# The second layer of a four-block transformer stack run in halves of two blocks, with layer norm and expert routing placed between expert tiles

## What is computed

```
x = x + 0.5 * ffn0(norm(x));  x = x + mamba(norm(x));  x = x + 0.5 * ffn0(norm(x))
x = x + 0.5 * moe(norm(x));   x = x + attention(norm(x));  x = x + 0.5 * moe(norm(x))

def moe(x):                       # 64 experts of width 88, top 8 of 64
    scores = sigmoid(x @ gate_w.T)            # [T, 64]
    # 8 groups of 8 experts; a group's value is the sum of its two best
    # keep the 4 best groups, then the 8 best experts, weights normalised * 2.5
    rw = route(scores, gate_bias)             # [T, 64], zero but for 8
    out = sum_e rw[:, e] * (silu(x @ Wg[e].T) * (x @ Wu[e].T)) @ Wd[e].T
    return out + shared(x)                    # one always-on expert, width 176
```

## Time and profile before

| | |
|---|---|
| time, three runs | 1789.91, 1790.04, 1793.42 us; median 1790.04 |
| the profiled execution | time 1788.16 us, span 1786.4 us |
| busy over the span | PE 1614.6 us (90%), DVE 1227.8 (69%), ACT 955.5 (53%), POOL 897.1 (50%) |
| mean granted PE clock | 0.947 of 2.4 GHz |
| DMA | 118.72 MB in 30035 packets |
| F1, mixer, F2 | 0 to 631.2 us of the span |
| E1 | 631.2 to 1070.7 |
| attention | 1070.7 to 1334.6 |
| E2 | 1334.6 to 1786.4 |

### The profile page before, as it was taken

How to read it: one execution, slowest core, us unless ns; L and a number is a source line. 1 busy time by engine, 2 the same in 40 slices (tenths; PEclk the granted TensorE clock), 3 DMA queues, 4 the chain that set the end, 5 groups by cost and what they waited for, 6 DMA issues and landing times.

```text
span 1786.4 us, 25495 instructions
## 1 busy us (share of the span) xinstructions
PE 1614.6 (90%) x6840; PEld 1208.8 (68%) x6840; DVE 1227.8 (69%) x2015; ACT 955.5 (53%) x1866; POOL 897.1 (50%) x786
## 2 busy tenths in 40 slices
PE   8997577787899975999999998999998699999998
PEld 6775323333377754888888876898875488888887
DVE  5555699999755564666666666787766466666666
ACT  4344645454334342565656555777763256556565
POOL 1001076666410042777777773434323277777776
PEclk9998789999899987999999998999997699999999
DMA  2000000000000003666667640000000367767765
GB/s 102 10 0 1 0 1 1 0 0 0 7 1 1 0 36 84 147 150 152 146 154 150 144 105 1 1 0 0 0 10 1 91 144 152 152 147 152 148 150 120
DMA packets 30035, 118.72 MB, mean 66 GB/s; under 512 B 5323, under 2 KB 17059, under 8 KB 18211
## 3 DMA queue, kind: packets, MB, share of 16 engines
q1 hardware_dynamic: 29987, 118.15, 29.8%
HBM read 116.03 MB, written 2.10 MB: 66 GB/s over the span
## 4 chain that ended last, share of the span: by engine, by line
PE 66%; DVE 3%; issue 2%; POOL 2%; ACT 2%; DMA 1%; POOLq 0%; DVEq 0%; SPq 0%; ACTq 0%
PE ps L219 19%; PE ps L220 18%; PE ps L221 18%; PE ps L1292 2%; PE ps L1277 1%; PE ps L1279 1%; PE ps L1278 1%; PE ps L643 1%; POOL m_hc L853 1%; PE ps L242 1%; DMA rwb<-rw_rows 1%; PE ps L255 1%; POOL e_lo L227 1%; PE ps L249 1%; PE ps L1280 1%
## 5 line engine op out<-in xcount | busy, mean ns | idle before, releaser
L227 POOL TENSOR_TENSOR e_lo<-e_h,e_hi 128x512 fp32r<-128x512 f32 (+1 forms) x368 | 478.5, 1300 | 259.3 <-ACT e_hi L224 252.2
L1160 DVE TENSOR_TENSOR ps<-e_s,ps 128x512 f32<-128x512 f32 x352 | 245.1, 696 | 239.4 <-PE ps L221 179.8
L985 ACT ACTIVATE e_s<-ps 128x512 f32<-128x512 f32 (+1 forms) x368 | 220.5, 599 | 324.6 <-PE ps L221 324.5
L219 PE MATMUL ps<-xn_hi,eh 128*128 128x512 f32 x704 | 280.6, 399 | 22.6 <-DVE ps L1160 22.6
L220 PE MATMUL ps<-xn_lo,eh 128*128 128x512 f32 x704 | 280.8, 399 | 0.0
L221 PE MATMUL ps<-xn_hi,el 128*128 128x512 f32 x704 | 276.4, 393 | 0.0
L1171 DVE TENSOR_TENSOR e_h<-ps,rwb 128x512 f32<-128x512 f32 x352 | 243.3, 691 | 44.7 <-DMA rwb<-rw_rows 21.0
L224 ACT ACTIVATE e_hi<-e_h 128x512 fp32r<-128x512 f32 (+1 forms) x368 | 229.0, 622 | 47.5 <-DVE e_h L1171 25.5
L853 POOL TENSOR_TENSOR m_hc<-m_h,m_c 128x512 f32<-128x512 f32 x128 | 172.8, 1350 | 124.9 <-DVE m_h L809 122.5
L643 PE MATMUL ps<-m_hc,const 128*128 128x512 f32 x256 | 149.6, 667 | 48.8 <-POOL m_hc L853 43.9
L219 PEld LDWEIGHTS ps<-xn_hi,eh 128*128 128x128 f32 x704 | 133.7, 190 | 55.0 <-DVE ps L1160 24.8
(11 more groups left out here) (239 smaller groups left out, 3180.5 us busy)
## 6 DMA issues: line engine op xcount, KB each, us to landing
rwb<-rw_rows SPq DMA_DIRECT2D x32, 704.0 KB
rwb<-rw_rows SPq DMA_DIRECT2D x40, 512.0 KB
e_raw<-in_experts SPq DMA_DIRECT2D x88, 192.0 KB, 5.5
rwb<-rw_rows SPq DMA_DIRECT2D x16, 640.0 KB
rwb<-rw_rows SPq DMA_DIRECT2D x24, 384.0 KB
rwb<-rw_rows SPq DMA_DIRECT2D x16, 448.0 KB
rwb<-rw_rows SPq DMA_DIRECT2D x16, 320.0 KB
rwb<-rw_rows SPq DMA_DIRECT2D x40, 128.0 KB
```

Of the source, the lines that this page charges most:

```text
L219: pe.matmul(out, w_hi, x_hi, start=start, stop=False, skip_group_check=True)
L227: return eng.tensor_tensor(lo, full, hi.bitcast(F32), ALU.subtract)
L985: act.activation(e_s[0:rows_, buf, :], ps[0:rows_, 4, :], ACT.Silu).then_inc(S["silu"], 1)
L1160: dve.tensor_tensor(ps[0:rows_, 6 + buf % 2, :], e_s[0:rows_, buf, :], ps[0:rows_, 5, :], ALU.mult).then_inc(S["gated"], 1)
```

## The change

The second layer no longer runs stage by stage over four blocks but half by half over two: E1A (blocks 0, 1), attention of blocks 0 and 1, E1B (blocks 2, 3), attention of 2 and 3, E2A (0, 1), E2B (2, 3), with a barrier after each; there are nine phases where there were six. Each chunk's weights are therefore loaded and split for every half again, 176 chunk loads where there were 88, into four slots of `e_raw`; a chunk now serves two tiles, and `rwb` of a chunk has 1024 columns (512 KB) where it had 2048. A half has 4 shared tiles and 88 expert tiles; the order of the last round is `CLOSING`, so that block 0's sum is whole two tiles before block 1's.

Layer norm and routing go to one block at a time and lie between tiles of another half, in functions `beside(t)` that are called after tile t on PE, ACT, DVE and POOL. Routing has 24 steps on [128, 256] tiles in five pieces (`route_pairs`, `route_groups`, `route_mask`, `route_top`, `route_weights`). E1A has beside it the norm of block 3 and the routing of blocks 2 and 3, E1B the norm and routing for E2 of blocks 0 and 1, E2A those of blocks 2 and 3, E2B nothing. Routing of blocks 0 and 1 for E1, and the logits of block 2, move into F2, whose loop over blocks is written out. The norm ahead of attention is made for a half's first block at the end of the expert half (`N`), for its second block inside attention. The attention weights' low halves are made by DVE in eight pieces of 288 columns (`attention_low`) at tiles 19 to 34 of E1A, the high halves by ACT in eight.

```diff
+        def route_pairs(dve, R, b):
+
+            dve.wait_ge(*R("scores", b + 1))
+            bias = rows[:, R_GB:R_GB + E].unsqueeze(1).broadcast_to([P, 4, E])
+            route_step(dve, R, b, 1, dve.tensor_tensor(r_c[:, :, :], r_s[:, b, :, :], bias, ALU.add))
+            if b:
+                dve.wait_ge(*R("rw_t", b))
+            lo, hi = r_c8[:, :, 0:4], r_c8[:, :, 4:8]
+            route_step(dve, R, b, 2, dve.tensor_tensor(of_groups(r_t, 0, 4), lo, hi, ALU.max))
+            route_step(dve, R, b, 3, dve.tensor_tensor(of_groups(r_u, 0, 4), lo, hi, ALU.min))
+            a0, a1 = halves(r_t, 0, 4)
+            m0, m1 = halves(r_u, 0, 4)
+            route_step(dve, R, b, 4, dve.tensor_tensor(of_groups(r_u, 4 * NGT, 2), a0, a1, ALU.min))
+            route_step(dve, R, b, 5, dve.tensor_tensor(of_groups(r_t, 4 * NGT, 2), a0, a1, ALU.max))
+            route_step(dve, R, b, 6, dve.tensor_tensor(of_groups(r_t, 6 * NGT, 2), m0, m1, ALU.max))
...
+                    if i and layer_ == 0:
+                        one_high(act, N, i - 1)
+                if R and i:
+                    route_scores(act, R, i - 1, 0)
+                if R and i >= 2:
...
+            def beside(t):
+
+                if first is None:
+                    return
+                if L and t == 1 and first in L[1]:
+                    one_mean(pe, L[0], first, 2)
+                if L and t == 2:
+                    one_mean(pe, L[0], second, 3)
+                if L and t == 5 and first in L[1]:
+                    one_var(pe, L[0], first, 2)
+                if L and t == 6:
+                    one_var(pe, L[0], second, 3)
+                if L and t == 9 and first in L[1]:
+                    one_spread(pe, L[0], first, 2)
+                if L and t == 10:
+                    one_spread(pe, L[0], second, 3)
+                if t == 14 and first in L[1]:
+                    pe.wait_ge(*L[0]("normed", first + 1))
+                    route_logits(pe, R, L[0], first, 2)
+                if t == 15:
+                    pe.wait_ge(*L[0]("normed", second + 1))
+                    route_logits(pe, R, L[0], second, 3)
+                if t == 24:
+                    pe.wait_ge(*R("scores", first + 1))
+                    route_turn(pe, R, first, 2)
+                if t == 34:
+                    pe.wait_ge(*R("scores", second + 1))
+                    route_turn(pe, R, second, 3)
+
+            pe.wait_ge(*R1("small_lo", 2))
+            for t in range(AHEAD):
...
                     expert_gate_up(i + (j + AHEAD) // PER, (j + AHEAD) % PER)
-                    expert_down(i, j, False)
+                    expert_down(i, j)
+                    if isinstance(i, int):
+                        beside(in_round(i, j))
+
+            begun = SIDE if ahead else 0
+            for i in range(begun):
...
+            def beside(t):
+                if first is None:
+                    return
+                if t == 4 and first in L[1]:
+                    one_square(act, L[0], first)
+                if t == 5:
+                    one_square(act, L[0], second)
+                if t == 7:
+                    if first in L[1]:
+                        one_deviation(act, L[0], first, 2)
+                    one_deviation(act, L[0], second, 3)
+                    load_table(act, ACT.Silu)
+                if t == 12 and first in L[1]:
+                    one_high(act, L[0], first)
+                if t == 13:
+                    one_high(act, L[0], second)
+                if t == 16:
+                    if first in L[1]:
+                        route_scores(act, R, first, 2)
+                    route_scores(act, R, second, 3)
+                    load_table(act, ACT.Silu)
+                if t == 26:
+                    route_rows(act, R, first, 2)
+                if t == 35:
+                    route_rows(act, R, second, 3)
+                if R is R1 and 17 <= t < 17 + ATT_PARTS:
+                    attention_high(act, t - 17)
...
+            def beside(t):
+                if first is None:
+                    return
+                if t == 3 and first in L[1]:
+                    one_centre(dve, L[0], first, 2)
+                if t == 4:
+                    one_centre(dve, L[0], second, 3)
+                if t == 8 and first in L[1]:
+                    one_diagonal(dve, L[0], first)
+                if t == 9:
+                    one_diagonal(dve, L[0], second)
+                if t == 11 and first in L[1]:
+                    one_normalise(dve, L[0], first, 2)
+                if t == 12:
+                    one_normalise(dve, L[0], second, 3)
+                if t in (17, 26):
+                    route_pairs(dve, R, first if t == 17 else second)
+                if t in (18, 27):
+                    route_groups(dve, R, first if t == 18 else second)
+                if t in (20, 29):
+                    route_mask(dve, R, first if t == 20 else second)
+                if t in (21, 31):
+                    route_top(dve, R, first if t == 21 else second)
+                if t in (23, 32):
+                    route_weights(dve, R, first if t == 23 else second)
+                if R is R1 and t in (19, 22, 24, 25, 28, 30, 33, 34):
...
+        def moe_store_rows(sp, R, half):
+            span_ = slice(2 * T * half, 2 * T * (half + 1))
+            sp.wait_ge(*R("rwt", 2 * half + 2))
+            sp.dma_start(d["rw_rows"][0 if R is R1 else 1, :, span_], rwt[:, span_]).then_inc(R[f"rw_out{half}"], 16)
...
+        def moe_load(sp, S, half, layer_, R, ahead):
+
+            for ch in range(SLOTS, CH):
+                sp.wait_ge(*S("wg_lo", ch - SLOTS + 1))
+                sp.wait_ge(*S("wd_lo", ch - SLOTS + 1))
+                moe_weights(sp, S, ch)
+                sp.wait_ge(*S("weighted", SHARED + 2 * (ch - SLOTS) + 2))
+                moe_row_weights(sp, S, half, layer_, ch)
+                if ahead and ch == 24:
+                    moe_store_rows(sp, R, ahead[0] // 2)
...
+            moe_pe(pe, E1B, 1, R2, (LN5A, (0, 1)), (0, 1), LN4B)
+            end_phase(pe)
+            start_phase(pe, 6)
+            att_pe(pe, LN4B, 1)
+            end_phase(pe)
+            start_phase(pe, 7)
+            moe_pe(pe, E2A, 0, R2, (LN5B, (2, 3)), (2, 3), None)
+            end_phase(pe)
+            start_phase(pe, 8)
+            moe_pe(pe, E2B, 1, R2, None, None, None)
             end_phase(pe)
 
         @block.scalar
```

More of the change, by code:

```diff
@@ L359, in one_var @@
             for t in range(4):
[L360 removed]
+                tt = slice(b * T + t * P, b * T + (t + 1) * P)
+                last = pe.matmul(ps[:, bank, t:t + 1], ln_t[:, tt], mean_w[:, 0:1], start=True, stop=True, skip_group_check=True)
             last.then_inc(L["var"], 1)
@@ new lines, in route_scores, with route_turn @@
+        def route_scores(act, R, b, bank):
+            act.wait_ge(*R("logits", b + 1))
+            act.activation(r_s[:, b, :, :].rearrange("p t e -> p (t e)"), ps[:, bank, 0:4 * E], ACT.Sigmoid).then_inc(R["scores"], 1)
+        def route_turn(pe, R, b, bank):
+            pe.wait_ge(*R("route", ROUTE_STEPS * (b + 1)))
+            for t in range(4):
+                last = pe.transpose(ps[0:E, bank, t * P:(t + 1) * P], r_t[:, t * E:(t + 1) * E], ident)
+            last.then_inc(R["rw_t"], 1)
@@ L898, in gate_up, with in_round, moe_pe @@
+        SHARED, PER, AHEAD, SLOTS = 4, 8, 3, 4
+        ROUNDS = CH // SLOTS
+        SIDE = 4
+        ORDERED = tuple((j // 2, j % 2) for j in range(PER))
+        CLOSING = ((0, 0), (0, 1), (1, 0), (1, 1), (2, 0), (3, 0), (2, 1), (3, 1))
+        FREE_BANKS = (2, 3)
+        def in_round(i, j):
+            return PER * i + SHARED + j
+        def moe_pe(pe, S, half, R, L, ahead, N):
+            first, second = ahead or (None, None)
             def gate_up(t, gh, gl, uh, ul, b, rows_):
+                blk = cut(2 * half + b)
@@ new lines, in round_ @@
+                    if j in (3, 5, 7) and not last:
+                        gate_up_high(i + 1, (j - 3) // 2)
+                    if j in (4, 6) and not last:
+                        down_high(i + 1, (j - 4) // 2)
+                    if isinstance(i, int) and not last:
+                        beside(t)
+            begun = SIDE if ahead else 0
+            for i in range(begun):
+                round_(i, False)
+            with act.Fori(begun, ROUNDS - 1) as i:
+                round_(i, False)
@@ L1071, in shared_gate, with moe_dve @@
+            begun = SIDE if ahead else 0
+            for i in range(begun):
+                round_(i, False)
+            with pool.Fori(begun, ROUNDS - 1) as i:
+                round_(i, False)
+            round_(ROUNDS - 1, True)
+            if N:
+                one_low(pool, N, 2 * half)
+        def moe_dve(dve, S, half, R, L, ahead, N):
+            first, second = ahead or (None, None)
             def shared_gate(t):
@@ L1147, in moe_dve, with tile @@
[L1147 to L1156 removed]
```

(15 more changed lines are left out.)

881 lines of the change are left out of this document (450 added, 431 removed).

## The result

The changed kernel takes 1844.25 us at the median of four runs (1839.23 to 1850.01), the kernel before 1791.73: a ratio of 1.0294, 95% interval 1.0258 to 1.0329. The change costs 52.5 us where I forecast 24. The direction was right and the time lies in the range, near its upper end, but the size is off by a factor of two.

The account below looks back on a forecast made before the run. Expert stages were taken as PE-bound while tiles flow, and bound by a DVE and DMA chain at their start. E1 +28.3, E2 -23.6, F2 +13, attention +7.1 gave +24.8 us: forecast 1814 us, range 1772 to 1848.

Parts of the forecast that it names:

- F2: Phase that takes on logits, transposes and routing: waits on ACT and DVE make it 13 us longer, 9 to 18.
- The pace: Expert halves: tiles stay 2.08 us apart in the loops, with no loss from POOL's work or weight loads.
- the bare half: E2B, with no norm or routing beside its tiles: 10.3 us beyond tile work, 201.7 us in all.
- TensorE's own side work: Mean, variance, spread, logits and transposes on PE: 5 us in E1A, 9.3 in E1B and in E2A.
- The sign that I gave for the first: Changed profile: PE idle before up matmuls, released by `gated`, near tiles 17 to 32, about 13 us a half.
- Insertions on DVE: Routing pieces between tiles: 4.0 us a block over the allowances, 3.3 from GpSimd; 13 us a half, 2 more in E1A.
- the allowance: DVE between tiles: a piece of 1.06 us costs nothing, or 0.66 us in the tile behind another piece.
- Norm: End of E1A and E1B: the first block's norm takes 9.5 us beyond the last tile's PE work, against 3 plain.
- Insertions on ACT: Tiles 7 and 16: ACT's waits and table loads idle PE 2.5 and 2.7 us, 5.2 a half in three halves.
- (a): Whole kernel: slower as summed, 1796 to 1834 us, with DVE and ACT stops of 3 to 9 us a block; chance 0.50.
- (b): Whole kernel faster as insertions hide: 1757 us without DVE's 41 and ACT's 15.6, 1785 with half removed; chance 0.26.
- (c): Expert loops: the pace falls through row weights, splits or POOL; 0.1 us a tile is 37 us, 1850; chance 0.15.

Follow-up runs that it names:

- E1A: Not a run: the changed kernel's phase with the expert tiles of blocks 0 and 1 in the second layer; with its attention it measured 378.5 us.
- E1B: Not a run: the changed kernel's phase with the expert tiles of blocks 2 and 3 in the second layer; with its attention it measured 378.6 us.
- wfirst: Changed kernel with the loads of E1A's first four chunks issued ahead of the store of the row weights: 1840.02 us, ratio 1.0272 to the kernel before.
- late_fine: Changed kernel with instructions that wait for TensorE put behind later tiles and routing cut into 17 pieces a block: 1772.95 us, ratio 0.9903 to the kernel before.
- thin: Changed kernel with GpSimd's low halves of expert weights cut to one column in four rounds of three halves: 1837.99 us, ratio 1.0257 to the kernel before.
- late: Changed kernel with each instruction that waits for TensorE put one to four tiles later, pieces uncut: 1817.06 us, ratio 1.0162 to the kernel before.
- fine: Changed kernel with a block's routing in 17 pieces, one a tile, turns and rows moved to match: 1794.88 us, ratio 1.0028 to the kernel before.
- best: late_fine with 21 routing pieces a block and E1A's first weights asked for ahead of the store: 1769.2 us, ratio 0.989 to the kernel before.

## Why the prediction was right and wrong

**Right.** F2 costs 11.1 us (13, range 9 to 18). The pace holds; so does the bare half, 199.1 us for 201.7. E1A's start waits 4.16 us for its weights (4), shown by wfirst. A half's attention with the rest of the norm ahead of it is 143.4 and 144.4 us, by my terms 142 (135.5, and 9.5 less the 3 of a plain end). TensorE's own side work, read off the gaps in late_fine (0.87 a mean or a spread, 0.89 a variance, 1.35 a set of logits, 0.45 a turn), is 4.9, 8.9 and 8.9 us a half, together 22.6 where I had 23.6. The mechanisms are those named: pieces longer than the gap before bank 5 is needed, and ScalarE's stops. The sign that I gave for the first came as given, TensorE idle before up matmuls some 13 us a half (12.0, 14.1 and 13.4), and still did not give the size: it is not the time that the stops cost.

**The step "Insertions on DVE" was mis-sized.** 39 us for the routing in three halves; 49.4 measured by profiled executions, 55.4 by medians. The pieces by themselves were nearly right (1.85, 1.35, 2.25, 1.50 and 1.75 us in F2, 8.7 for my 8.5), and so was the allowance: the tile with a piece of length p takes 1.37 + p (5.24 us for 3.87 of steps), the one behind 1.75, so p less 1.06 is lost, and p less some 0.7 where a piece stands in the tile before too (my 0.66). Six of the missing 10 us are the lock with GpSimd: the row-derived 3.3 us a block was 4.3, 25.8 us over six blocks in place of 19.8. Most of it lands on the path, because each piece is already past its allowance; thin shows one piece where it does not. The rule of the Trainium skill (SBUF — State Buffer, "Who interferes with whom") by itself gave 6 us a block. The trace agrees with it where the two meet (thin), and the 4.3 measured lie between my reading of the rows and that sum. The other 4 us are a wait that I put at nothing: the 1.25 us at tile 26 for the turns of the block before, 3.7 us in three halves. The tile in which it falls takes 5.32 us, 1.37 and the 3.95 of its piece, wait included, so it is lost whole. It is there in late and gone in fine, late_fine and best, where the turn stands well ahead of the second block.

**The steps "Norm" and "Insertions on ACT" missed waits.** Without the routing steps the surplus is 59.7 us (17.9, 20.3 and 21.6), where my terms without routing give 44.2: 15.5 us. ScalarE's stops are 18.6 us of waiting at TensorE (15.6 forecast): the third is one I did not have, the rows at tile 35, which wait for the turned block and put two gated products 4.39 us apart. VectorE's centre and normalise steps stand before the next gated product until TensorE has made the mean: 7.0 us (3 forecast). The last 9.5 are left over by subtraction (TensorE's own work was 1 less than forecast). 3.3 of them are there without any work beside the tiles: the 87 tiles of E2B took 182.1 us and not 181. Another part is TensorE's clock behind ScalarE's stops: without the routing steps tiles 9 to 11 took 9.53 us in E2A at 0.83 and 8.27 in E1B at 1.00, which is the 1.3 us between the two halves. That term was not in my sum at all. The rest stays open.

**Of the rivals**, (a) has the mechanisms, and both the stops (49.4 and 18.6 us over six blocks, 11 a block) and the time lie above its bounds of 9 us and 1834. (b) was half right about what decides it. The insertions do hide, all but 6 to 10 us of the routing, once a piece is hardly longer than the gap; the single bank 5 did not forbid it, as I had argued. The total of 8.5 us against "4.6 us of idle in seven tiles" was the wrong comparison, since there are 88 tiles. (c) did not happen: its 1850 is nearer to the result than my 1814, but the pace did not fall. That the range held the time is owed to (c), which widened it, and so to luck.

## What to carry to other kernels

Price an insertion by its longest piece and not by its total: below the gap that one tile leaves it is almost free, above it nearly all counts, stretching by a neighbour's lock too. In a program of in-order engines, place a side instruction by where its input is made in the *producer's* program: an engine that runs three tiles behind hands it over one to four tiles later than the same number in the source suggests. The same holds for a tile that a second piece of work writes again: ask when the first one's reader is done. Here these two rules, with the same work in the same stages, turned 3% slower into 1.1% faster.

## What the runs showed of the hardware, unexpected

- The granted clock of a stretch rose from 0.92 to 1.00 with 74 unread products in a half's waits, and the stretch stayed at 45 us: a low clock in a stretch with waits is a sign of waiting, and a cost only where TensorE is the bound (8.26 and 10.65 us for the same 32 instructions at 1.00 and 0.73).
- A table load on ScalarE, which is busy for 64% of late_fine's E1B, cost 1.1 us by the medians of all twelve (0.8 to 1.4), of its 1.28, once nothing was waited for in front of it.
- A VectorE step of 128x4 was drawn out from 0.16 to 1.22 us, a step of 128x32 from 0.19 to 1.20: the shortest steps lose the most by GpSimd's lock in proportion. A reduction of 128x256 (0.42), which reads one input, kept its length beside GpSimd in all six blocks.
